# Relation maps by copies inside SBUF, ten chunks per loop turn and interleaved expert products, in a one-core attention and mixture-of-experts kernel

## The chip, the cores and the metric

One core of one Trainium2 chip runs the whole program. The metric is the device time of one execution in microseconds (us); times are medians over runs.

## What is computed

One pre-norm layer over 4096 tokens of width 256, 16 heads of 16, in fp32:

```python
q, k, v = (xn @ W.T + b for each)                      # (4096, 16, 16)
li = xn @ rel_W[:, :d].T;  lj = xn @ rel_W[:, d:].T    # 3 relations
probs = softmax(li[i] + lj[j] + rel_b)                 # per pair of tokens
bias = probs @ logical_bias.T                          # per head
gate = sigmoid(xn @ gate_W.T + gate_b)
w = softmax(q k^T / 4 + gate * bias)
x = x + (w @ v) @ Wo.T + bo
logits = layernorm(x) @ Wg;  top 2 of 8 experts, softmax over the two
x = x + sum_k weight_k * (relu(xn @ W1[e] + b1[e]) @ W2[e] + b2[e])
```

## The kernel before, in words

The program has three parts, each a block in which the five engines run lists of their own, tied by semaphores.

`project_inputs` (to 287 us) normalises x and makes q, k, v, gates and relation logits. VectorE splits q and k into two fp16 parts, and SP, the queue that issues nearly all DMAs, writes q and the coefficients to DRAM (L205, L217) and k into the stack `kst` in SBUF (L220). VectorE's third group of splits waits for all those stores (L309), since it writes over their source.

`attend` takes 32 chunks of 128 queries. A chunk has 32 steps of 128 keys (jt), and eight units of 512 keys. For a step TensorE forms the scores of two halves of eight heads in PSUM (`sc`): per half eight matmuls of q and k (L764) and eight of the relation terms (L775), the latter with the keys' relation maps `rst` as the stationary side (112 rows: high and low fp16 parts of two maps for 16 queries, and rows of ones that carry the negative row maximum) and the coefficients `cm` as the moving one. Eight blocks of 16 queries need a matmul each; block b holds queries 16b to 16b+15, so its output is, per head, a run of 16 neighbouring floats. ScalarE exponentiates (L653) and TensorE multiplies by the values (L811). In the same steps TensorE computes score maxima for later chunks (L786), two heads at a time, which VectorE reduces (L685); 16 of a chunk's 64 products are done two chunks ahead (AHEAD).

The relation maps of a chunk are 16 pieces (8 units x 2 kinds), each made by two clamps on VectorE (L677, from the key logits `dj` that SP loads per unit, L476), two exponentials on ScalarE (L631), a sum on GpSimd (L590), a logarithm and an exponential on ScalarE (L637, L639), and a rounded copy and a remainder on GpSimd (L594, L596). All 16 of a chunk are made during the chunk before; those of chunk 0 before the first scores, between the maxima products (L718 to L722). SP writes the two parts to DRAM, re-laid, in `sp_write_r` (L490) and reads a unit back in two transfers in `sp_read_r` (L500, L501) when one of the two unit buffers is free, that is when the scores before it are done (L540). GpSimd waits for the stores before it fills `rhi` again (L592). Per chunk SP also loads q (L466), sends the row maxima in eight copies (`sp_m`, L515), the output (L507) and loads the constants of the chunk after next (L480, L482).

`in_chunks` (L78) runs the chunks on every engine as a loop of 15 turns over two chunks; the last two chunks stand behind it as straight code.

`experts` adds the attention output, routes the tokens and runs 23 blocks of 512 gathered tokens. In a block TensorE does eight up products (L1344), turns the next block's tokens (L1289), and does the four output tiles of the block before (L1358), 24 matmuls each. ScalarE applies relu (L1268) and makes the high parts of the weights (L1238), VectorE splits the hidden values (L1208, L1210), splits x (L1146) and adds the bias to the output tiles (L1222), all splits of one block before the biases of the last; GpSimd makes the low parts of the weights (L1033). The output tiles have two PSUM banks, so TensorE can be two tiles ahead of VectorE.

## Time and profile before

| | us |
|---|---|
| median of 3 runs | 5311.16 |
| lowest and highest | 5309.63, 5318.84 |
| the profiled execution: its time | 5305.37 |
| its span in the trace | 5303.6 |

The page gives busy time per engine over the span: TensorE 4609.0 us, its weight loads 3497.3, VectorE 4010.2, ScalarE 3394.0, GpSimd 2102.8. A busy share is an average over stages; it says which engine a stage leans on, and the rows in order of time say who waits for whom. Durations of neighbouring matmuls overlap, so a step is read from start to start.

### The profile page before, as it was taken

What the parts mean: (1) busy time and instruction counts of PE and PEld (TensorE: products, weight loads), DVE (VectorE), ACT (ScalarE), POOL (GpSimd) and SP (SyncE); (2) the same over time, 40 slices, a digit from 0 to 9 for tenths busy, and PEclk for the clock granted to TensorE, in tenths of its full rate; (3) what the DMA queues carried; (4) which work ended last, traced back from release to release, by engine and by line L of the source; (5) the groups of instructions that cost most, each with busy time, mean ns of one, the idle gap of its engine ahead of it and who ended that gap; (6) DMA issues with size and microseconds to landing.
All of it is one profiled execution on the core that took longest, in us unless ns stands there. A gap on an engine that the chain in (4) does not pass through costs nothing. (4 is left out here: it accounts for less than half of the span.)

```text
span 5303.6 us, 184408 instructions
## 1 busy us (share of the span) xinstructions
PE 4609.0 (87%) x74128; PEld 3497.3 (66%) x74128; DVE 4010.2 (76%) x6341; ACT 3394.0 (64%) x4457; POOL 2102.8 (40%) x1811
## 2 busy tenths in 40 slices
PE   4548999999999999999999999999999983688882
PEld 3216777777777777777777777777777773466662
DVE  7288888888888888888888888888888613566663
ACT  0136877878787878787787878787878840233330
POOL 4043444444444444444444444444444413323234
PEclk8758999999999999999999999999999985789996
DMA  2634555555555555555555555555555552333323
GB/s 58 101 95 119 150 137 151 149 139 150 141 149 145 150 137 148 142 146 137 151 151 138 151 142 150 144 151 136 148 140 147 143 161 89 115 115 116 113 105 107
DMA packets 455013, 710.53 MB, mean 134 GB/s; under 512 B 138664, under 2 KB 306472, under 8 KB 425792
## 3 DMA queue, kind: packets, MB, share of 16 engines
q1 hardware_dynamic: 447936, 681.00, 47.0%
q0 software_dynamic: 6144, 16.79, 1.0%
q8 instruction: 622, 10.19, 0.8%
q14 instruction: 311, 2.55, 0.1%
HBM read 506.30 MB, written 184.93 MB: 130 GB/s over the span
## 5 line engine op out<-in xcount | busy, mean ns | idle before, releaser
L685 DVE TENSOR_REDUCE b_mxp<-b_mx 128x1 f32<-128x512 f32 x4096 | 2624.7, 683 | 541.0 <-PE b_mx L786 466.3
L653 ACT ACTIVATE b_pr<-b_sc 128x1024 f32<-128x1024 f32 x2048 | 1987.7, 1021 | 773.1 <-PE b_sc L775 772.5
L764 PE MATMUL b_sc<-b_qm,kst 128*128 128x128 f16 x16384 | 1276.4, 221 | 86.6 <-issue 82.0
L775 PE MATMUL b_sc<-b_cm,b_rst 112*128 112x128 f16 x16384 | 1275.8, 221 | 1.3 <-issue 1.3
L764 PEld LDWEIGHTS b_sc<-b_qm,kst 128*128 128x128 f16 x16384 | 977.8, 98 | 284.8 <-ACT b_pr L653 174.0
L775 PEld LDWEIGHTS b_sc<-b_cm,b_rst 112*128 112x128 f16 x16384 | 976.0, 98 | 227.7 <-issue 227.6
L811 PE MATMUL b_acc<-b_pr,vp 128*32 128x128 f32 x32768 | 1110.9, 276 | 0.5 <-issue 0.5
L811 PEld LDWEIGHTS b_acc<-b_pr,vp 128*32 128x32 f32 x32768 | 835.3, 110 | 231.6 <-ACT b_pr L653 195.4
L594 POOL CAST b_rhi<-b_ex 128x512 f16<-128x512 f32 x512 | 321.4, 628 | 1570.5 <-ACT b_ex L639 785.7
L786 PE MATMUL b_mx<-kst,b_qx 64*128 64x512 f16 x4096 | 822.8, 398 | 120.8 <-DVE b_mxp L685 116.0
L590 POOL TENSOR_TENSOR b_ex<-b_ex 128x512 f32<-128x512 f32 x512 | 658.0, 1285 | 528.7 <-ACT b_ex L631 528.1
L677 DVE TENSOR_SCALAR b_dl<-b_dj,b_const 128x512 f32<-128x512 f32 x1024 | 772.4, 756 | 5.0 <-DMA b_dj<-key_logits 3.7
L596 POOL TENSOR_TENSOR b_rlo<-b_ex,b_rhi 128x512 f16<-128x512 f32 x512 | 604.8, 1181 | 40.9
L631 ACT ACTIVATE b_ex<-b_dl 128x512 f32<-128x512 f32 x1024 | 588.2, 627 | 35.7 <-DVE b_dl L677 34.6
L786 PEld LDWEIGHTS b_mx<-kst,b_qx 64*128 64x128 f16 x4096 | 197.5, 93 | 373.4 <-DVE b_mxp L685 170.0
L1268 ACT ACTIVATE c_h<-c_ps,c_b1b 128x512 f32<-128x512 f32 x184 | 124.2, 689 | 425.1 <-PE c_ps L1344 283.2
L1358 PE MATMUL c_ps<-c_w2p,c_a 128*128 128x256 f16 x2208 | 294.6, 302 | 104.8 <-DVE c_y L1222 104.8
L637 ACT ACTIVATE b_ex<-b_ex 128x512 f32<-128x512 f32 x512 | 323.0, 631 | 91.6 <-POOL b_ex L590 91.4
L1358 PEld LDWEIGHTS c_ps<-c_w2p,c_a 128*128 128x128 f16 x2208 | 237.4, 108 | 158.3 <-DVE c_y L1222 110.9
L639 ACT ACTIVATE b_ex<-b_ex 128x512 f32<-128x512 f32 x512 | 322.3, 630 | 16.2
L1033 POOL TENSOR_TENSOR c_w1p<-c_w1r,c_w1p 128x2048 f16<-128x2048 f32 x22 | 90.2, 4100 | 448.5 <-ACT c_w1p L1238 448.5
L1344 PE MATMUL c_ps<-c_xT,c_w1p 128*128 128x512 f16 x1104 | 247.5, 385 | 11.4 <-issue 9.9
(143 smaller groups left out, 2016.8 us busy)
## 6 DMA issues: line engine op xcount, KB each, us to landing
b_dj<-key_logits SPq DMA_DIRECT2D x256, 768.0 KB, 7.5
b_rst<-relation_parts SPq DMA_DIRECT2D x256, 512.0 KB, 4.8
relation_parts<-b_rhi SPq DMA_DIRECT2D x512, 128.0 KB
relation_parts<-b_rlo SPq DMA_DIRECT2D x512, 128.0 KB
b_rst<-relation_parts SPq DMA_DIRECT2D x256, 256.0 KB, 5.3
c_w1r<-in_L_ffn_W_dram SPq DMA_DIRECT2D x23, 1024.0 KB, 4.8
c_w2r<-in_L_ffn_W_dram SPq DMA_DIRECT2D x23, 1024.0 KB, 4.8
expert_tokens<-c_zeros SPq DMA_DIRECT2D x23, 512.0 KB, 7.0
```

The source lines that it names most:

```text
L590: nc.gpsimd.tensor_tensor(ex[:, k, 0], ex[:, k, 0], ex[:, k, 1], ALU.add).then_inc(s["sum_ready"], 1)
L596: nc.gpsimd.tensor_tensor(rlo[:, k], ex[:, k, 0], rhi[:, k], ALU.subtract).then_inc(s["lo_ready"], 1)
L631: nc.scalar.activation(ex[:, k, n], dl[:, k, n], ACT.Exp, scale=sign).then_inc(s["e_ready"], 1)
L637: nc.scalar.activation(ex[:, k, 0], ex[:, k, 0], ACT.Ln, bias=1.0).then_inc(s["ln_ready"], 1)
L653: nc.scalar.activation(pr[:, jt % 2, half, :], sc[:, half].rearrange("p a b -> p (a b)"), ACT.Exp).then_inc(s["p_ready"], 1)
L677: nc.vector.tensor_scalar(dl[:, k, n], dj[:, u % 2, d], const[:, par, b:b + 1], limit, ALU.add, op).then_inc(s["d_ready"], 1)
L685: nc.vector.tensor_reduce(mxp[:, head, part:part + 1], mx[:, (bank + ab) % MX_RING, :], AX.X, ALU.max).then_inc(s["mx_used"], 1)
L764: pe.matmul(sc[:, half, side, p * P:p * P + P], kst[:, pair, jt * P:jt * P + P], qm[:, par, pair, :, side * IS:side * IS + IS], start=(p = ...
L775: ins = pe.matmul(out, rst[:, u % 2, b, j0:j0 + P], cm[:, par, half, b], start=False, stop=(b % (NB // 2) == NB // 2 - 1), skip_group_chec ...
L786: pe.matmul(mx[:, (bank + ab) % MX_RING, :], qx[rows, par, pair, :], kst[rows, pair, j0:j0 + 512], start=True, stop=True).then_inc(s["mx_r ...
L811: ins = pe.matmul(acc[32 * (h % 4):32 * (h % 4) + 32, h // 4, :], vp[:, jt, VW * h:VW * h + 32], pr[:, jt % 2, half].rearrange("p (a h i) ...
L1358: ins = pe.matmul(ps[:, 4 + d % 2, 0:D], hT[:, (b - 1) % 2, hp, f, t * P:t * P + P], w2p[:, (b - 1) % 2, wp, f, :], start=(f == 0 and hp = ...
```

## The change

In the attention part the relation maps no longer go through DRAM. GpSimd writes them into four slots, and per piece SP copies six times from SBUF to SBUF straight into `rst` (two sides of 64 queries, three row groups). The pieces are made two units ahead of their use, not a chunk ahead; chunk 0 has four made before the first scores and the rest in its steps. For the copies each block takes every fourth query of its side, so the relation matmul writes every fourth float of `sc`. The key load moves behind the copies and four units ahead, clamps run one step earlier, coefficients are loaded in two halves in unit 7, row maxima go in two copies. The loop has three turns of ten chunks; two chunks stand behind it. In the projection part six stores take the place of 48. In the experts two up products alternate with one output tile on TensorE, and VectorE's splits with the biases; the weights' high parts are made after the second and fourth relu in place of the fourth and sixth.

```diff
+R_AHEAD, D_AHEAD = 4, 3
+CLAMP_SLOT, ACC_SLOT = 0, 1
+UNROLL, LOOPS = 10, 3
...
-    with eng.Fori(0, (NT - 2) // 2) as pair:
-        chunk(pair * 2, 0, pair + 1, False)
-        chunk(pair * 2 + 1, 1, pair + 1, False)
-    chunk(NT - 2, 0, NT // 2, False)
-    chunk(NT - 1, 1, NT // 2, True)
+    with eng.Fori(0, LOOPS) as turn:
+        for n in range(UNROLL):
+            chunk(turn * UNROLL + n, n % 2, turn * (UNROLL // 2) + n // 2 + 1, False)
+    for c in range(LOOPS * UNROLL, NT):
+        chunk(c, c % 2, c // 2 + 1, c == NT - 1)
...
-                    for b in range(NB):
-                        sp.dma_start(c_dram[:, part, k].rearrange("x (i b) h -> b i x h", b=NB)[b],
-                                     t[BI * b:BI * b + BI, k]).then_inc(stored, 16)
...
+        rhi = sb("rhi", [P, 4, JU], F16)
+        rlo = sb("rlo", [P, 4, JU], F16)
...
+            for side in range(2):
+                sp.dma_start(cval[0:M_ROW, par, NB // 2 * side:NB // 2 * side + NB // 2, :],
+                             c_dram[bass.ds(x, 1)].rearrange("o a k (s i b) h -> s (o a k) i (b h)", s=2, b=NB // 2)[side]
+                             ).then_inc(s[f"cval_in{par}"], 16)
...
-        def sp_write_r(sp, x, g):
-
-            u, k = g // 2, g % 2
-            sp.wait_ge(s["lo_ready"], 16 * x + g + 1)
+        def sp_r(sp, x, u, k):
+
+            sp.wait_ge(s["lo_ready"], 16 * x + 2 * u + k + 1)
             waited(sp)
-            for part, t in ((0, rhi), (1, rlo)):
-                sp.dma_start(r_dram[bass.ds(x, 1), u, part, k].rearrange("o (i b) j -> b (o i) j", b=NB), t[:, k]).then_inc(
-                    s[f"r_out{k}{u % 2}"], 16)
-
-        def sp_read_r(sp, x, u, written):
-
-            for k in range(2):
-                sp.wait_ge(s[f"r_out{k}{u % 2}"], 32 * written)
-            waited(sp)
-            src = r_dram[bass.ds(x, 1), u].rearrange("o a k (i b) j -> (o a k i) (b j)", b=NB)
-            dst = rst[:, u % 2].rearrange("r b j -> r (b j)")
-            sp.dma_start(dst[0:64], src).then_inc(s[f"r_in{u % 2}"], 16)
-            sp.dma_start(dst[64:96], src[0:32]).then_inc(s[f"r_in{u % 2}"], 16)
+            for side in range(2):
+                for part, t in enumerate((rhi, rlo, rhi)):
+                    row = 32 * part + BI * k
+                    sp.dma_start(rst[row:row + BI, u % 2, NB // 2 * side:NB // 2 * side + NB // 2, :],
+                                 t[IS * side:IS * side + IS, 2 * (u % 2) + k, :]).then_inc(s[f"r_in{u % 2}"], 16)
...
-            for b in range(NB):
-                sp.dma_start(cval[M_ROW:M_ROW + BI, par, b], m16[BI * b:BI * b + BI, :]).then_inc(s["m_in"], 16)
+            for side in range(2):
+                sp.dma_start(cval[M_ROW:M_ROW + BI, par, NB // 2 * side:NB // 2 * side + NB // 2, :],
+                             m16[IS * side:IS * side + IS, :]).then_inc(s["m_in"], 16)
...
                 for u in range(UNITS):
-                    if u > 0 or not (isinstance(c, int) and c == 0):
-                        sp.wait_ge(s["scores_ready"], STEPS * c + max(SPU * u, 1))
-                        waited(sp)
-                    newer = 0 if last else len(range((u + 1) % 2, u - 1, 2))
-                    if u + 1 < UNITS:
-                        sp_read_r(sp, c, u + 1, UNITS // 2 * (c + 1) + newer - (1 if u == 0 else 0))
-                    elif not last:
-                        sp_read_r(sp, c + 1, 0, UNITS // 2 * (c + 1) + newer)
-                    if not last and (more or u + 1 < UNITS):
-                        sp.wait_ge(s["d_ready"], 32 * (c + 1) + 4 * u)
-                        waited(sp)
-                        sp_dj(sp, (u + 1) % UNITS)
+                    sp.wait_ge(s["scores_ready"], STEPS * c + max(SPU * u, 1))
+                    waited(sp)
                     for k in range(2):
-                        if u == 0:
-                            sp_write_r(sp, c, 2 * UNITS - 2 + k)
+                        if u + 1 < UNITS:
+                            sp_r(sp, c, u + 1, k)
                         elif not last:
-                            sp_write_r(sp, c + 1, 2 * u - 2 + k)
+                            sp_r(sp, c + 1, 0, k)
                         if u == 0 and k == 0 and not last:
                             sp_q(sp, c + 1, 1 - par)
                         if u == M_UNIT and k == 0 and not last:
                             sp_m(sp, c + 1, 1 - par)
+                    if u + 4 < UNITS or not last:
+                        sp.wait_ge(s["d_ready"], 32 * c + 4 * u + 12)
+                        waited(sp)
+                        sp_dj(sp, (u + 4) % UNITS)
                     if u == 1:
                         sp_att(sp, c)
                         if more:
                             sp.wait_ge(s["c_made"], 2 * c + 2)
                             waited(sp)
                             sp_qx(sp, c + 2, par)
-                            sp_consts(sp, c + 2, par)
+                    if u + 1 == UNITS and more:
+                        sp_consts(sp, c + 2, par)
...
-            r_stored(pool, x, u - 1, k)
+            if not (isinstance(x, int) and x == 0 and u < 2):
+                pool.wait_ge(s[f"r_in{u % 2}"], 192 * (UNITS // 2 * x + u // 2))
...
+                for turn in range(2 * UNITS):
+                    g = turn + R_AHEAD
+                    if g < 2 * UNITS:
+                        pool_r(pool, c, g)
+                    elif not last:
+                        pool_r(pool, c + 1, g - 2 * UNITS)
+                    if turn in C_MAPS and not last:
+                        pool_c(pool, c + 1, 1 - par, nth + par, C_MAPS.index(turn))
...
+                    g = jt // 2 + R_AHEAD
+                    if g < 2 * UNITS:
+                        (act_r_inv if jt % 2 else act_r_exp)(act, c, g)
+                    elif not last:
+                        (act_r_inv if jt % 2 else act_r_exp)(act, c + 1, g - 2 * UNITS)
...
-                if n % 3 == 0 and n // 3 < 2 * UNITS:
+                if n % 2 == 0 and n < 2 * R_AHEAD:
                     for k in range(2):
-                        dve_d(dve, 0, 0, 1, n // 3, k)
+                        dve_d(dve, 0, 0, 1, n // 2, k)
...
+                        if slot == CLAMP_SLOT:
+                            g, k = R_AHEAD + (jt + D_AHEAD) // 2, (jt + D_AHEAD) % 2
+                            if g < 2 * UNITS:
+                                dve_d(dve, c, par, nth, g, k)
+                            elif not last:
+                                dve_d(dve, c + 1, 1 - par, nth + par, g - 2 * UNITS, k)
...
-                side, i0 = b // (NB // 2), b % (NB // 2) * BI
-                out = sc[:, half, side, :].rearrange("p (h i) -> p h i", h=HH)[:, :, i0:i0 + BI]
+                side, part = b // (NB // 2), b % (NB // 2)
+                out = sc[:, half, side, :].rearrange("p (h i b) -> p h i b", h=HH, b=NB // 2)[:, :, :, part]
...
+                for i in range(BT):
+                    if b < NBLK:
+                        if b >= 2 and i == 0:
+                            dve.wait_ge(s["down_done"], BT * (b - 1))
+                        for f in range(i * FT // BT, (i + 1) * FT // BT):
+                            split_h(dve, b, f)
+                    if b + 1 < NBLK and i == 2:
                         split_x(dve, b + 1)
-                if b > 0:
-                    par, nth = (b - 1) % 2, (b - 1) // 2
-                    dve.wait_ge(s[f"w2_in{par}"], 32 * nth + 32)
-                    if nth:
-                        dve.wait_ge(s[f"y_out{par}"], 16 * nth)
-                    for t in range(BT):
-                        d = BT * (b - 1) + t
-                        dve.wait_ge(s["down_done"], d + 1)
-                        nc.vector.tensor_tensor(y[:, par, t], ps[:, 4 + d % 2, 0:D], b2b[:, (b - 1) % 4],
-                                                ALU.add).then_inc(s["y_done"], 1)
+                    if b > 0:
+                        add_bias(dve, b - 1, i)
 
             for g in range(GROUPS):
...
-                    if f == 3 and b + 1 < NBLK:
+                    if f == 1 and b + 1 < NBLK:
...
-                    if f == 5:
+                    if f == 3:
...
+                for i in range(BT):
+                    if b < NBLK:
+                        if i == 0:
+                            pe.wait_ge(s["w1_lo"], b + 1)
+                            pe.wait_ge(s["x_lo"], KC * (b + 1))
+                        for f in range(i * FT // BT, (i + 1) * FT // BT):
+                            up(pe, b, f)
+                    if b + 1 < NBLK and i == 1:
                         turn_x(pe, b + 1)
-                if b > 0:
-                    pe.wait_ge(s["w2_lo"], b)
-                    pe.wait_ge(s["h_split"], 2 * FT * b)
-                    for t in range(BT):
-                        d = BT * (b - 1) + t
-                        if d >= 2:
-                            pe.wait_ge(s["y_done"], d - 1)
-                        for f in range(FT):
-                            for hp, wp in parts:
-                                ins = pe.matmul(ps[:, 4 + d % 2, 0:D], hT[:, (b - 1) % 2, hp, f, t * P:t * P + P],
-                                                w2p[:, (b - 1) % 2, wp, f, :], start=(f == 0 and hp == 0 and wp == 0),
-                                                stop=(f == FT - 1 and wp == 1))
-                        ins.then_inc(s["down_done"], 1)
+                    if b > 0:
+                        if i == 0:
+                            pe.wait_ge(s["w2_lo"], b)
+                            pe.wait_ge(s["h_split"], 2 * FT * b)
```

## Rows read from the trace of the kernel before

**Rows 1.** Windows: us, busy of PE, PEld, DVE, ACT, POOL, clock, DMA.

```profile
800.00:1800.00 1000.00, 968.02 (x17753) 739.75 (x17754) 856.48 (x1346) 791.51 (x1042) 432.33 (x408) 0.99 0.54 146
...
4750.00:4809.00 59.00, 49.15 (x310) 37.10 (x309) 38.07 (x45) 20.66 (x26) 17.59 (x5) 0.91 0.33 112
```

**Rows 2.** Timeline, TensorE, chunk 30: start us, us, engine, line, operation.

```profile
4130.93 1.08 PE L811 MATMUL b_acc<-b_pr,vp 128*32 128x128 f32 x32
...
4134.59 1.08 PE L811 MATMUL b_acc<-b_pr,vp 128*32 128x128 f32 x32
```

**Rows 3.** Waits, whole span: us in total, times, longest us.

```profile
POOL b_rhi L594 <- DMA relation_parts<-b_rlo: 784.9, 218, 7.4
...
PE b_sc L764 <- issue: 82.0, 14, 6.0
```

**Rows 4.** Timeline, TensorE, expert blocks.

```profile
4770.72 10.52 PE L1344 MATMUL c_ps<-c_xT,c_w1p 128*128 128x512 f16 x48
4781.08 1.04 PE L1289 MATMUL c_ps<-c_ident,c_xb 128*128 128x128 f32 x8
...
4792.29 7.06 PE L1358 MATMUL c_ps<-c_w2p,c_a 128*128 128x256 f16 x48 [4.94 <-DVE c_y L1222]
...
4828.75 10.52 PE L1344 MATMUL c_ps<-c_xT,c_w1p 128*128 128x512 f16 x48
...
5193.96 15.89 PE L1358 MATMUL c_ps<-c_w2p,c_a 128*128 128x256 f16 x144 [1.29 <-DVE c_y L1222]
```

**Rows 5.** Timeline, TensorE, a loop turn.

```profile
1158.94 1.08 PE L811 MATMUL b_acc<-b_pr,vp 128*32 128x128 f32 x32
1166.02 1.03 PE L764 MATMUL b_sc<-b_qm,kst 128*128 128x128 f16 x8 [6.00 <-issue]
...
1170.73 1.08 PE L811 MATMUL b_acc<-b_pr,vp 128*32 128x128 f32 x32
```

**Rows 6.** Timeline, VectorE and GpSimd in one of these blocks.

```profile
4779.20 3.83 DVE L1208 CAST c_a<-c_h 128x512 f16<-128x512 f32 x1 [1.22 <-ACT c_h L1268]
4783.07 4.45 DVE L1210 TENSOR_TENSOR c_a<-c_h,c_a 128x512 f16<-128x512 f32 x1
...
4787.89 0.69 DVE L1210 TENSOR_TENSOR c_a<-c_h,c_a 128x512 f16<-128x512 f32 x1
...
4778.66 4.10 POOL L1033 TENSOR_TENSOR c_w1p<-c_w1r,c_w1p 128x2048 f16<-128x2048 f32 x1 [21.26 <-ACT c_w1p L1238]
```

**Rows 7.** Timeline, SP and VectorE in the projection stage.

```profile
128.17 17.30 SPq L205 DMA_DIRECT2D c_values<-a_chi  x32
...
136.08 0.69 DVE L313 TENSOR_TENSOR a_x_room<-a_qk,a_part_hi 128x512 f16<-128x512 f32 x1
...
200.93 0.43 DVE L311 CAST a_part_hi<-a_qk 128x512 f16<-128x512 f32 x1 [50.71 <-DMA q_stacks<-a_x_room]
```

**Rows 8.** Timeline, VectorE before the first scores.

```profile
301.49 1.22 DVE L677 TENSOR_SCALAR b_dl<-b_dj,b_const 128x512 f32<-128x512 f32 x2
```

**Rows 9.** Timeline of SP, then its issues: KB each, median us to landing.

```profile
1131.73 5.86 SPq L515 DMA_DIRECT2D b_cval<-b_m  x8
...
1162.94 2.00 SPq L466 DMA_DIRECT2D b_qm<-q_stacks  x2
...
kst<-a_part_hi SPq DMA_DIRECT2D x32, 128.0 KB, 5.4
b_cval<-b_m SPq DMA_DIRECT2D x256, 0.5 KB, 2.1
```

**Rows 10.** By line: times, duration ns min/median/max, first and last start us.

```profile
L764 PE MATMUL b_sc<-b_qm,kst x16384: 217/219/314, 425.4 to 4318.1; 128*128 128x128 f16 x200
...
L775 PE MATMUL b_sc<-b_cm,b_rst x16384: 216/219/314, 426.2 to 4318.5; 112*128 112x128 f16 x200
...
L1358 PEld LDWEIGHTS c_ps<-c_w2p,c_a x2208: 95/98/152, 4578.8 to 5209.5; 128*128 128x128 f16 x184
...
L1344 PEld LDWEIGHTS c_ps<-c_xT,c_w1p x1104: 140/143/168, 4540.8 to 5186.8; 128*128 128x128 f16 x184
```

More of the change, by code:

```diff
@@ L608, in _ @@
             pool.wait_ge(s["eye_made"], ROWS // BI + 1)
-            for g in range(2 * UNITS):
+            for g in range(R_AHEAD):
                 pool_r(pool, 0, g)
@@ L614, in chunk, with act_r_exp @@
             def chunk(c, par, nth, last):
-                if not last:
-                    for g in range(2 * UNITS):
-                        pool_r(pool, c + 1, g)
-                        if g in C_MAPS:
-                            pool_c(pool, c + 1, 1 - par, nth + par, C_MAPS.index(g))
+                for turn in range(2 * UNITS):
[6 more added lines that the diff above has]
+                        pool_c(pool, c + 1, 1 - par, nth + par, C_MAPS.index(turn))
             in_chunks(pool, chunk)
-        def act_r_exp(act, x, u, k):
-            g = 16 * x + 2 * u + k
+        def act_r_exp(act, x, n):
+            g, k = 16 * x + n, n % 2
             act.wait_ge(s["d_ready"], 2 * g + 2)
@@ L643, in _ @@
             nc.scalar.preload_act_table_set("natural_log_exp_and_others")
-            for u in range(UNITS):
-                for k in range(2):
-                    act_r_exp(act, 0, u, k)
-                    act_r_inv(act, 0, u, k)
+            for g in range(R_AHEAD):
+                act_r_exp(act, 0, g)
+                act_r_inv(act, 0, g)
             def chunk(c, par, nth, last):
@@ L725, in _ @@
                 dve_pair(dve, 1, n, 2 * PAIRN + 2 * n)
-            for k in range(2):
-                dve_d(dve, 1, 1, 1, 0, k)
+            for n in range(D_AHEAD):
+                dve_d(dve, 0, 0, 1, R_AHEAD + n // 2, n % 2)
             def chunk(c, par, nth, last):
@@ L1290, in turn_x, with up, down @@
                 ins.then_inc(s["x_turned"], 1)
+        parts = ((0, 0), (1, 0), (0, 1))
+        def up(pe, b, f):
+            n = b * FT + f
+            if n >= 4:
+                pe.wait_ge(s["relu_done"], n - 3)
+            for c in range(KC):
+                for wp, xp in parts:
+                    ins = pe.matmul(ps[:, n % 4, :], w1p[:, b % 2, wp, c, f:F:FT], xT[:, b % 2, xp, c],
+                                    start=(c == 0 and wp == 0 and xp == 0), stop=(c == KC - 1 and xp == 1))
+            ins.then_inc(s["up_done"], 1)
+        def down(pe, b, t):
+            d = BT * b + t
+            if d >= 2:
+                pe.wait_ge(s["y_done"], d - 1)
+            for f in range(FT):
+                for hp, wp in parts:
+                    ins = pe.matmul(ps[:, 4 + d % 2, 0:D], hT[:, b % 2, hp, f, t * P:t * P + P],
+                                    w2p[:, b % 2, wp, f, :], start=(f == 0 and hp == 0 and wp == 0),
+                                    stop=(f == FT - 1 and wp == 1))
+            ins.then_inc(s["down_done"], 1)
         @block.tensor
```

109 lines of the change are left out of this document (41 added, 68 removed).

## The prediction

> **What bounds the kernel now.** I read the busy time by stretch first, then the waits, then one step of TensorE in order of time. In the thousand microseconds from 800 on TensorE is busy 968, VectorE 856, ScalarE 792 and GpSimd 432, with the clock at 0.99 (the 2.4 GHz level) and the DMA engines half busy [rows 1]: attention is TensorE's. Two neighbouring steps of one chunk show the pace: the product with the values (L811) of one step starts 3.66 us after that of the step before, and nothing in between waits [rows 2]; 1024 such steps are about 3750 us of the span of 5303.6. Where TensorE does stop, the list of waits names two kinds. It waited 14 times for "issue", 5.9 us on average [rows 3], and there are 14 jumps back in a loop of 15 turns over two chunks. And GpSimd waited 785 us for the relation parts to reach DRAM [rows 3], but GpSimd is the idlest engine here and TensorE's waits don't name it: that stall goes with the change and is worth nothing by itself. The expert stage is another matter. There TensorE stands 4.94 us in every block for VectorE's bias addition (L1222), and two blocks take 58.03 us [rows 4].
>
> The profiled execution took 5305.4 us (span 5303.6), 0.1% under the median of 5311.2 us of three runs, so I subtract its durations from the median. A measurement of this kernel can tell about 0.2%, 11 us, from no change.
>
> **Loop turns.** At a turn the value products of two neighbouring steps start 11.79 us apart instead of 3.66, with 6.00 us of it "issue" and the first matmuls behind it at about double their usual time [rows 2, 5]. So a turn costs 8.1 us. Ten chunks a turn leave two jumps back of fourteen: 12 x 8.1 = 97 us. The bounds are 12 x 5.9 = 71 (the stop alone) and 100. The straight-line end of the present program, chunks 30 and 31, is where the two rows of the 3.66 us pace stand [rows 2], so long unlooped code runs at full pace.
>
> **Experts.** Today TensorE does a block's eight up products in 10.36 us, transposes (1.0 us), starts down and stops after the second output tile, because VectorE is to add the bias only after all its splits of the next hidden block. VectorE is late because two of its instructions took 3.83 and 4.45 us, beside GpSimd's weight splits of 4.1 us each; alone the second one takes 0.69 [rows 4, 6]. Alternating two up products with one down product gives VectorE the time of 5.3 us per pair of splits and one bias. TensorE's own work per block is 10.36 + 1.0 + 96 x 0.110 = 22.0 us (0.110 from the 144 last matmuls in 15.9 us) [rows 4]. VectorE is busy 38.07 us in two blocks, the long holds included: 19 a block [rows 1], still under 22. The tightest place is the x split, now put before the bias of the third tile while ScalarE copies x only after its eighth relu: going through it by these durations, x is ready about when the next block's first product wants it, and 0.2 to 1 us per block is lost. I take 22.6 against 29.0: 22 x 6.4 = 141, less about 4 at the ends, 137 us. Bounds: 95 (25 us a block) and 150. The weight splits move earlier (after f = 1 and 3); their loads are issued in the block before, some 15 us ahead, and stay covered.
>
> **Projection stage.** The coefficient stores take 32 x 0.54 us on SP, 48 of them 26 us, and then the q stores run until VectorE, 50.7 us idle, may go on at 200.93 [rows 7]. Six stores in place of 48 free 42 x 0.54 = 22.7 us of SP. But the q stores need the first eight tiles, finished at 136.8, so they start at 137 and not at 154: 17 us, and everything behind follows SP. The data moved is the same in as many pieces, and may slow the q stores: 16 us, between 5 and 23.
>
> **Start of attention.** Before the first scores VectorE works through 128 maxima with 16 pairs of clamps between them, 1.22 us a pair [rows 8]. Four pairs are left, twelve go into chunk 0, where TensorE is the bound and the same clamps ran in every chunk: 12 x 1.22 = 14.6, less one clamp that is put ahead of the first scores: 14 us, between 10 and 18.
>
> **Relation copies.** Per unit of 512 keys (four steps, 14.6 us) SP now issues 12 copies and one key load instead of six transfers and one. The nearest row to a copy inside SBUF is the 8 small ones of the row maxima, 5.86 us or 0.73 each, landing after 2.1 us; a 128 KB one lands after 5.4 [rows 9]. Twelve cost 8.8 us, and with the key load 9.3 of 14.6: SP keeps up. What is late next is the last copy of a unit. TensorE needs it 16.7 us after the buffer is free (four steps plus the part of a step that leads up to L775). In most units it lands at 12 to 13. In unit 6 it stands behind the row maxima, whose wait is now in front of it rather than behind the reads, and lands near 15. In unit 0 SP starts 3 us later (it waits for one half step more), the two loads of q (2.0 us) are between the copies [rows 9], and the sum 3.0 + 4.4 + 2.3 + 4.4 + 2.5 = 16.6 has no slack. I charge 0.3 us a chunk, 10 us; bounds 0 and 40. GpSimd's new wait, on copies of two units before, is met when it is asked. In the last chunk ScalarE now has maps to make where it had none: 2.9 us of work a step (0.79 of 3.66 [rows 1, 2]) against a TensorE step that there has no maxima products, four of 512 columns, 0.21 us each at 2.4 GHz (an estimate), so 2.8. 24 such steps give 2 us, 0 to 5. Two row-maximum copies in place of eight are behind other work.
>
> **Costed at nothing.** The key load (L476) now stands behind the copies, 10 to 13 us into a unit; VectorE's clamps want it six steps, 22 us, after the unit began, so TensorE's pace covers it until SP is 4 us behind. The loads of the constants and coefficients (three more issues) go from unit 1 to unit 7, still a chunk ahead of their use, and there SP has 5 us left. The clamps run one step earlier and ask for maps that ScalarE made two steps before. The copy of the accumulator keeps its place behind the last maxima product. If SP or VectorE lose these 4 to 5 us, the cost is rival 2's.
>
> **Sum.** 97 + 137 + 16 + 14 - 10 - 2 = 252 us: 5311 - 252 = 5059 us.
>
> **Rival 1, slower: the strided score write.** The relation matmul wrote runs of 16 neighbouring floats in PSUM and now writes every fourth float, 16 bytes apart. No row shows a matmul that does this. Two rows bound it. For nothing lost: L775 already breaks its output into runs, and its median is 219 ns, the same as L764's unbroken one [rows 10]. For a loss: on the reading side, a weight load with elements 16 bytes apart (L1344) takes 143 ns against 98 for a packed one (L1358) [rows 10]. If the write pays the same 45 ns on the engine that is the bound, 16384 x 45 ns = 737 us, and the time is 5796. It decides the sign from 252 / 16384 = 15 ns a matmul on. I take no cost, because the row of the same instruction and the same target is nearer than a load from SBUF; chance 0.16. The Trainium skill (Advanced Engine Details and Errata, PSUM Cachelines) speaks against this change: any non-contiguous access pattern is said to slow matmuls significantly, with every two neighbouring elements wanted together. By its first form L775 should be slow already, and the row says it isn't; its second form, pairs, no row here tests, and by it the result would be this rival.
>
> **Rival 2: SP becomes the clock of attention.** If a copy costs 1.2 us on SP rather than 0.73, a unit needs 12 x 1.2 + 0.8 = 15.2 us against 14.6, and unit 0 comes 5 us late: 256 x 0.6 to 32 x 5, about 150 us, time 5210. At 0.9 only unit 0 is late, by 2 us, and the time is near 5120. For it speaks that the q loads took 1.0 us each on SP [rows 9]; against it, that these copies have fixed addresses, like the row maxima's. Chance 0.13.
>
> **Rival 3: VectorE is held by GpSimd and bounds the experts.** With both long holds [rows 6] inside the x split's stretch a block takes 25 us: 22 x 2.4 = 53 less gained, 5112. Chance 0.11.
>
> **Rival 4: the loop does not do what it says.** If the stop comes back in the straight code as often as before, 97 us are missing: 5156. The pace in chunk 30 speaks against it. Chance 0.05.
>
> **Numbers.** The forecast has 0.52 and 0.03 are for what I don't see. The range takes the forecast's bounds (5311 less 290, and less about 125 when each term is poor) and rivals 2 to 4: 5020 to 5210. Left out are rival 1 and the 0.03. Faster 0.82, same 0.02, slower 0.16.
>
> **What would show it.** Right: two waits for issue of about 6 us at TensorE, 11.8 us between the value products there; first scores some 30 us earlier; no wait of L1358 for L1222 and about 22.6 us from block to block; copies of about 0.7 us each on SP; L775 still at 219 ns and a step of 3.66 us. Wrong: L775 longer or a step over 4 us (rival 1), TensorE waiting for the copied maps at the first or seventh unit (rival 2), VectorE's splits late before an up or down product (rival 3).

## The result and the profile after

The changed kernel takes 5853.6 us (median of 4 runs, 5850.5 to 5857.5) against 5312.4 of the kernel before: ratio 1.102, 95% interval [1.100, 1.104]. It is 541 us slower. The forecast was 5059, its range ended at 5210, and rival 1, the strided score write at 5796, is what happened. (A product here is one matmul of TensorE, PE in the views; PEld is its weight load.)

The windows of the changed kernel show what [rows 1] showed before; the second one is one expert block (columns as in [rows 1], then the busy share of the DMA engines and GB/s):

```profile
800.00:1800.00 1000.00, 1000.00 (x15054) 786.44 (x15054) 740.10 (x1140) 693.88 (x884) 364.10 (x345) 1.00 0.38 94
5331.76:5353.67 21.91, 21.91 (x152) 17.01 (x153) 16.68 (x23) 10.04 (x12) 8.30 (x2) 1.00 0.45 151
```

TensorE is busy all of the thousand microseconds, and 15054 products fit where 17753 did. VectorE, ScalarE, GpSimd and the DMA engines are all less busy than before, and the granted clock is no lower (1.00 against 0.99). So TensorE's own work became slower. The view by line says which of its products:

```profile
L762 PE MATMUL b_sc<-b_cm,b_rst x16384: 274/314/502, 408.6 to 5021.1; 112*128 112x128 f16 x200
...
L762 PEld LDWEIGHTS b_sc<-b_cm,b_rst x16384: 95/139/232, 408.5 to 5021.0; 112*128 112x128 f16 x200
...
L751 PE MATMUL b_sc<-b_qm,kst x16384: 219/219/395, 407.8 to 5020.3; 128*128 128x128 f16 x200
```

The score product (now L751) has its old median of 219 ns, the relation product (L762) went from a median of 219 to 314 ns [rows 10]. Durations of neighbouring products overlap, so the price is read from the timeline of TensorE, from start to start; [rows 2] have the same pair of value products before. The changed kernel:

```profile
2001.23 1.05 PE L762 MATMUL b_sc<-b_cm,b_rst 112*128 112x128 f16 x8
2002.07 0.65 PE L751 MATMUL b_sc<-b_qm,kst 128*128 128x128 f16 x8
2002.56 1.04 PE L762 MATMUL b_sc<-b_cm,b_rst 112*128 112x128 f16 x8
2003.53 0.39 PE L773 MATMUL b_mx<-kst,b_qx 64*128 64x512 f16 x2
2003.85 1.08 PE L798 MATMUL b_acc<-b_pr,vp 128*32 128x128 f32 x32
...
2008.36 1.08 PE L798 MATMUL b_acc<-b_pr,vp 128*32 128x128 f32 x32
```

The kernel before, between the two value products of [rows 2]:

```profile
4132.82 0.62 PE L775 MATMUL b_sc<-b_cm,b_rst 112*128 112x128 f16 x8
4133.28 0.61 PE L764 MATMUL b_sc<-b_qm,kst 128*128 128x128 f16 x8
4133.73 0.61 PE L775 MATMUL b_sc<-b_cm,b_rst 112*128 112x128 f16 x8
4134.27 0.39 PE L786 MATMUL b_mx<-kst,b_qx 64*128 64x512 f16 x2
```

A step is 4.51 us instead of 3.66. The two groups of eight relation products take 0.84 and 0.97 us to the next product's start, where they took 0.46 and 0.54: that is 0.81 of the 0.85 us, and the other 0.04 stand at the score group between them. Put on the 16 relation products of a step it is 0.85 / 16 = 53 ns each, which about doubles the distance between their starts. Over 1024 steps that is 870 us.

The spans add up. From the first relation product to the last the attention stage took 3892.3 us before (426.2 to 4318.5 [rows 10]) and 4612.5 now, 720 more. The stretch ahead of it is 17.6 us shorter, the stretch behind it 154.8 (985.1 before, 830.3 now): 720 - 18 - 155 = 548, and the spans differ by 547.8. The 720 is 870 less 150: from the starts of the 1024 value products I worked out how much each step takes over its ideal length (3.66 us before, 4.51 now, and 0.48 more in the one step of a chunk that holds four transposes), and the sum over the chunks fell from 161 us to 11. Below this is called the count over the ideal step. Of the 161, 112 were the loop turns, of which 10 are left; the other 49 were small waits that a slower TensorE no longer has.

### The profile page after: what moved, and what is told of

The parts are those of the page before. It is cut to its first block and busy times, and to the rows that moved or that the text cites. A ratio compares the mean times of both kernels' runs of the same rounds, so it can differ in the third digit from the quotient of the medians.

```text
span 5851.4 us, 182716 instructions
## 1 busy us (share of the span) xinstructions
PE 5392.3 (92%) x74128; PEld 4210.1 (72%) x74128; DVE 4050.4 (69%) x6341; ACT 3500.4 (60%) x4457; POOL 2087.7 (36%) x1811
## 5 line engine op out<-in xcount | busy, mean ns | idle before, releaser
L640 ACT ACTIVATE b_pr<-b_sc 128x1024 f32<-128x1024 f32 x2048 | 2098.5, 1025 | 1487.0 <-PE b_sc L762 1482.6
L762 PE MATMUL b_sc<-b_cm,b_rst 112*128 112x128 f16 x16384 | 2138.9, 310 | 0.0
L762 PEld LDWEIGHTS b_sc<-b_cm,b_rst 112*128 112x128 f16 x16384 | 1621.2, 129 | 222.9 <-issue 222.9
L751 PE MATMUL b_sc<-b_qm,kst 128*128 128x128 f16 x16384 | 1304.1, 222 | 5.7 <-issue 5.7
L751 PEld LDWEIGHTS b_sc<-b_qm,kst 128*128 128x128 f16 x16384 | 1062.4, 103 | 203.1 <-ACT b_pr L640 188.0
L579 POOL CAST b_rhi<-b_ex 128x512 f16<-128x512 f32 x512 | 312.8, 611 | 1802.7 <-ACT b_ex L627 1070.1
L663 DVE TENSOR_SCALAR b_dl<-b_dj,b_const 128x512 f32<-128x512 f32 x1024 | 824.9, 807 | 61.4 <-ACT b_ex L619 57.9
L581 POOL TENSOR_TENSOR b_rlo<-b_ex,b_rhi 128x512 f16<-128x512 f32 x512 | 593.9, 1160 | 40.9
L1307 PE MATMUL c_ps<-c_w2p,c_a 128*128 128x256 f16 x2208 | 255.4, 273 | 0.0
L1307 PEld LDWEIGHTS c_ps<-c_w2p,c_a 128*128 128x128 f16 x2208 | 216.0, 98 | 36.0
L1296 PEld LDWEIGHTS c_ps<-c_xT,c_w1p 128*128 128x128 f16 x1104 | 154.9, 145 | 87.3 <-issue 21.2
```

Source lines behind the costliest of these rows:

```text
L581: nc.gpsimd.tensor_tensor(rlo[:, slot], ex[:, k, 0], rhi[:, slot], ALU.subtract).then_inc(s["lo_ready"], 1)
L640: nc.scalar.activation(pr[:, jt % 2, half, :], sc[:, half].rearrange("p a b -> p (a b)"), ACT.Exp).then_inc(s["p_ready"], 1)
L663: nc.vector.tensor_scalar(dl[:, k, n], dj[:, u % 2, d], const[:, par, b:b + 1], limit, ALU.add, op).then_inc(s["d_ready"], 1)
L751: pe.matmul(sc[:, half, side, p * P:p * P + P], kst[:, pair, jt * P:jt * P + P], qm[:, par, pair, :, side * IS:side * IS + IS], start=(p = ...
L762: ins = pe.matmul(out, rst[:, u % 2, b, j0:j0 + P], cm[:, par, half, b], start=False, stop=(b % (NB // 2) == NB // 2 - 1), skip_group_chec ...
L1296: ins = pe.matmul(ps[:, n % 4, :], w1p[:, b % 2, wp, c, f:F:FT], xT[:, b % 2, xp, c], start=(c == 0 and wp == 0 and xp == 0), stop=(c == K ...
```

## Experiments

**Is it the write?** Theory W says that a write at every fourth float costs TensorE 53 ns a product. Theory R keeps the write innocent: copies into the product's operand now run beside it, and its weight loads went from 98 to 139 ns too. The first run puts the write back and leaves the relation term on queries that it doesn't belong to; but for that and a scale in the exponent it is the changed kernel:

```diff
-                out = sc[:, half, side, :].rearrange("p (h i b) -> p h i b", h=HH, b=NB // 2)[:, :, :, part]
+                out = sc[:, half, side, :].rearrange("p (h i) -> p h i", h=HH)[:, :, BI * part:BI * part + BI]
```

> The changed kernel with only the relation product's write put back to runs of 16 neighbouring floats, nothing else adjusted: the relation term lands on other queries, and the exponent of the scores is scaled by 1/16 to keep it finite. This is all the rest of the change without the strided write. Theory W: 5854 - 870 = about 4985 us, a step of 3.66. Theory R: 5854, the relation product at 272 ns or more. My sum of the other parts alone would give 5059.

Measured: 5042.0 us, ratio 0.949 [0.947, 0.951]. The second does the opposite, in the kernel before:

```diff
-                out = sc[:, half, side, :].rearrange("p (h i) -> p h i", h=HH)[:, :, i0:i0 + BI]
+                out = sc[:, half, side, :].rearrange("p (h i b) -> p h i b", h=HH, b=NB // 2)[:, :, :, part]
```

> The kernel before with only the write of the relation product changed to every fourth float; relation maps still go through DRAM, the loop and the experts are the old ones. The relation term lands on other queries than it should, and the exponent of the scores is scaled by 1/16 to keep it finite; the work is the same. Theory W: the relation product goes from 219 to 272 ns, the step from 3.66 to 4.51, the time from 5312 to 5312 + 1024 x 0.85 = about 6180 us, less what the loop turns' stop overlaps (6100 to 6190). Theory R: nothing changes, 5312.

Measured: 6119.6, ratio 1.152 [1.150, 1.154]. By line, the run with runs of 16:

```profile
L762 PEld LDWEIGHTS b_sc<-b_cm,b_rst x16384: 95/98/152, 406.8 to 4204.4; 112*128 112x128 f16 x200
L762 PE MATMUL b_sc<-b_cm,b_rst x16384: 216/219/314, 406.9 to 4204.5; 112*128 112x128 f16 x200
```

and the kernel before with the strided write:

```profile
L775 PEld LDWEIGHTS b_sc<-b_cm,b_rst x16384: 95/139/233, 426.3 to 5133.5; 112*128 112x128 f16 x200
L775 PE MATMUL b_sc<-b_cm,b_rst x16384: 274/314/502, 426.4 to 5133.7; 112*128 112x128 f16 x200
```

Both numbers of the changed kernel, 314 for the product and 139 for its weight load, come with the write and go with it, whatever the copies do. Theory R is dead. The second run is 805 us over its kernel before by the medians and 813 by the profiled spans; 870, less the 49 of small waits, which vanish here too, less 8 by which the turns are shorter (104 us for 112) is 813. The first run was expected 57 us lower, since 5854 - 870 forgets that those waits come back (51 us of them by the count): 5042 is what the rest of the change gives.

**How far apart may the floats be?** Two kernels change the pattern alone (with the same scale in the exponent), to pairs of neighbours with 24 bytes between, and to every second float:

```diff
-                out = sc[:, half, side, :].rearrange("p (h i b) -> p h i b", h=HH, b=NB // 2)[:, :, :, part]
+                out = sc[:, half, side, :].rearrange("p (h i b t) -> p h i b t", h=HH, b=NB // 2, t=2)[:, :, :, part, :]
...
-                out = sc[:, half, side, :].rearrange("p (h i b) -> p h i b", h=HH, b=NB // 2)[:, :, :, part]
+                out = sc[:, half, side, :].rearrange("p (h a i b) -> p h a i b", h=HH, a=2, b=2)[:, :, part // 2, :, part % 2]
```

> The changed kernel with the relation product writing pairs: two neighbouring floats, then the next pair 32 bytes on (the term lands on other queries, exponent scaled by 1/16). If neighbouring pairs are enough for full speed: the time of the run with runs of 16, about 4985 us. If each break in the run costs the same (64 breaks instead of 128), half the loss stays: about 5420. If anything short of long runs costs all: 5854.

> The changed kernel with the relation product writing every second float (8 bytes apart) instead of every fourth (the term lands on other queries, exponent of the scores scaled by 1/16). If what counts is that two neighbouring floats are written together: the full loss, 5854. If the loss grows with the distance: between 5042 and 5854, near 5450.

Measured: pairs 5036.9 (ratio 0.948 [0.946, 0.949]), every second float 5854.9 (1.101 [1.100, 1.103]). With pairs the product's row reads 216/219/314, with every second float

```profile
L762 PE MATMUL b_sc<-b_cm,b_rst x16384: 274/314/502, 408.5 to 5023.0; 112*128 112x128 f16 x200
```

Of these patterns it is a step, not a slope. 64 breaks in the run cost nothing while each piece is two floats; distances of 8 and of 16 bytes between single floats cost the same 53 ns. The second form of the rule in the Trainium skill (Advanced Engine Details and Errata, PSUM Cachelines), that neighbouring elements are wanted in twos, holds to the nanosecond; its first form, that any non-contiguous pattern slows a product, does not, by the pairs and by the runs of 16.

**Can the order be had at the other end?** The strided write was there to match queries, since the copies give each block every fourth query: one copy of 64 neighbouring partitions leaves query 4 x row + block in each block. The write can be whole if the score product reads q in that order instead, and VectorE undoes the order in its copy of the accumulator (the diff shows the read alone):

```diff
-                              qm[:, par, pair, :, side * IS:side * IS + IS], start=(p == 0), stop=False,
+                              qm[:, par, pair, :, side * IS:side * IS + IS].rearrange("p a (i b) -> p a b i", b=NB // 2), start=(p == 0), stop=False,
```

> The changed kernel with one thing different: the relation product writes runs of 16 neighbouring floats again. So that its queries still meet the right scores, the score product reads q in the order (block, row) instead of (row, block), a moving operand whose fp16 elements stand 8 bytes apart, and VectorE's copy of the accumulator puts the queries back in their order. Everything else of the change stays. Theory W (the write at every fourth float costs TensorE 53 ns a product, 0.85 us in each of 1024 steps): the step falls from 4.51 to 3.66 us and the time to 5854 - 870 = about 4985 us, if reading q at a distance of 8 bytes is free. If that read costs what the write did (the 45 ns or more per product), the time stays near 5850 and the longer product is now that of the scores. Theory R (the product is slow because copies into its operand run beside it): no change for the relation product, 5854.

Measured: 5876.1, ratio 1.106 [1.104, 1.108]. The loss moved to the other product:

```profile
L752 PEld LDWEIGHTS b_sc<-b_qm,kst x16384: 95/113/152, 405.3 to 5040.7; 128*128 128x128 f16 x200
L752 PE MATMUL b_sc<-b_qm,kst x16384: 268/288/314, 405.3 to 5040.8; 128*128 128x128 f16 x200
...
L763 PE MATMUL b_sc<-b_cm,b_rst x16384: 217/219/314, 406.2 to 5041.3; 112*128 112x128 f16 x200
```

A step is 4.53 us, 55 ns a score product more than 3.66. Single fp16 elements 8 bytes apart, as the moving operand, cost what single floats cost on the writing side. Is it pairs here as well? The write stays at runs of 16, and the diff shows the read alone:

```diff
-                              qm[:, par, pair, :, side * IS:side * IS + IS], start=(p == 0), stop=False,
+                              qm[:, par, pair, :, :].rearrange("p a (n w) -> p (a n) w", w=4)[:, :, 0:2], start=(p == 0), stop=False,
```

> The changed kernel with the relation product writing runs of 16, and the score product reading pairs of neighbouring fp16 elements, 4 bytes, one pair every 8 bytes (it reads other queries than it should, exponent scaled by 1/16). In contig_correct the read of single fp16 elements 8 bytes apart cost as much as the strided write. If pairs of elements are enough on this side too: 5042. If 4 bytes of each 8 are too little: 5850, a score product of 272 ns.

Measured: 5055.4, ratio 0.951 [0.950, 0.953]; the score product is at 217/218/314 ns. Pairs of fp16 elements, 4 bytes of every 8, are read at nearly full speed: the usual step is 3.68 us where after_contig has 3.66, about 1 ns a product and 18 us in all, which covers the 13 us between the two runs. So the loss comes from the pattern with which TensorE touches single elements. The scaled exponent has no part in it: contig_correct and the complete versions below have no such scale, and their relation products stand at 219 ns. One thing was not tried: all these writes add to what stands in PSUM already, and whether a product that only writes pays the same is open.

**The two large terms alone.** The kernel before with the new loop (`UNROLL, LOOPS = 10, 3` and the new `in_chunks`), and the kernel before with the new expert stage:

> The kernel before with only the loop changed: ten chunks in a turn and three turns. My sum: two turns left of fourteen, 97 us less: 5314 - 97 = 5217. Rival, from the profile of the changed kernel with runs of 16, where small stops of TensorE for issue of 0.6 to 3 us stand scattered through the long body: those stops belong to the long body itself and give back some 30 us: 5245. Rival 4 of the prediction (stops come back as often): 5314.

> The kernel before with only the expert stage changed: one down product after every two up products, VectorE's bias additions between its splits, weight splits earlier. My sum: 22.6 us a block instead of 29.0, 137 us less: 5177. By the block of 21.91 us in the trace of the changed kernel: 22 x (29.0 - 21.9) = 156 less, 5158. Rival 3 (VectorE held by GpSimd, 25 us a block): 5230.

Measured: loop 5233.5, ratio 0.985 [0.984, 0.987], 79 us less; experts 5156.3, ratio 0.970 [0.969, 0.972], 156 us less. The timeline of TensorE in the experts' run:

```profile
4702.94 2.75 PE L1309 MATMUL c_ps<-c_xT,c_w1p 128*128 128x512 f16 x12
4705.53 2.78 PE L1320 MATMUL c_ps<-c_w2p,c_a 128*128 128x256 f16 x24
...
4724.85 2.75 PE L1309 MATMUL c_ps<-c_xT,c_w1p 128*128 128x512 f16 x12
```

A block is 21.91 us, without a wait. In the loop's run a turn is

```profile
1630.88 1.08 PE L812 MATMUL b_acc<-b_pr,vp 128*32 128x128 f32 x32
1636.45 1.03 PE L765 MATMUL b_sc<-b_qm,kst 128*128 128x128 f16 x8 [4.49 <-issue]
1641.17 1.07 PE L812 MATMUL b_acc<-b_pr,vp 128*32 128x128 f32 x15
```

10.29 us from value product to value product. By the count over the ideal step, the turns went from 112 to 14 us, 98 saved, but all the other steps together from 49 to 72. I took this for stops of the long body itself (there are scattered ones of 0.6 to 2 us), but 15 of the 23 us stand at the 27th to 29th step of a chunk, and at the 28th TensorE waits for ScalarE's exponentials: 11 times by the profile, against 2 in the kernel before. In chunk 2 GpSimd waits 3.75 us for the row maxima at its first coefficient product (L581), ScalarE 3.03 us for the relation sum behind it (L638), TensorE 1.38 us for ScalarE. That chain comes back below; it is in the kernel before too, and why it costs more with the long loop is not shown. The 79 us lie between my sum (97) and the rival of that expectation (some 30 given back, about 69). Of the 266.5 us between the profiled spans of the kernel before (5303.6) and of after_contig (5037.1), the turns gave 100, the stretch behind attention 152.5, the stretch before it 19.3, and all other steps lost 5: 267.

**A complete version without strides in TensorE's products.** The order has to be made off TensorE's path. ScalarE writes q in the order (block, row) when it leaves PSUM in the projection stage; VectorE restores the order once per chunk in its copy of the accumulator. The bounds of the shift follow q's order (three loads of constants instead of one), and the row maxima need eight copies again instead of two:

```diff
+                    if m < 2:
+                        dst = dst.rearrange("p (s b i) -> p s i b", s=8, b=4)
+                        src = src.rearrange("p (s i b) -> p s i b", s=8, b=4)
...
+            nc.vector.tensor_copy(oT[:, :, :].rearrange("p g (s i b) -> p (g s) b i", s=2, b=NB // 2),
+                                  acc[:, :, :].rearrange("p g (s b i) -> p (g s) b i", s=2, b=NB // 2)).then_inc(s["acc_read"], 1)
```

> A complete version of the change without a strided access in any product of attention. The queries are put in the order (block, row) once, where ScalarE writes q in the projection stage; the relation maps and coefficients keep their order, so that the relation product writes runs of 16 neighbouring floats and the copies within SBUF stay 64 neighbouring partitions each. VectorE's copy of the accumulator restores the order of the outputs, the constants are loaded by three transfers instead of one, and the row maxima by eight copies again instead of two. Theory W: the time of the changed kernel with runs of 16, 5042 us, plus at most 10 for eight maxima copies in unit 6: 5040 to 5052. If a strided access anywhere else in the kernel costs (ScalarE's writes of q at 16 bytes, VectorE's copy), it shows as a longer projection stage or a longer last step of a chunk, up to 20 us more.

Measured: 5118.8, ratio 0.963 [0.962, 0.965], 67 us over the top of what was expected. The timelines of SP and of TensorE in chunk 6 show why, first SP in the seventh unit, then TensorE at the start of the eighth:

```profile
1237.59 5.59 SPq L509 DMA_DIRECT2D b_cval<-b_m  x8
1243.37 0.59 SPq L494 DMA_DIRECT2D b_rst<-b_rhi  x1
```

```profile
1249.84 1.03 PE L769 MATMUL b_sc<-b_cm,b_rst 112*128 112x128 f16 x8 [2.10 <-DMA b_rst<-b_rhi]
```

The eight maxima copies stand between the two halves of the relation copies for the eighth unit; the last half starts 5.8 us late, and TensorE waits 1.1 to 3.8 us in nearly every chunk, 62 us in the first 30 chunks. That is the place where the prediction said twelve copies would land "near 15" of 16.7 us, with two maxima copies in front. So I moved the eight behind the relation copies (`if u == M_UNIT and k == 1`):

> As runs_of_16, with one step moved on SP: in the seventh unit the eight copies of the row maxima stand behind the twelfth copy of the relation maps, not behind the sixth. In the trace of runs_of_16 TensorE waits 1.1 to 3.8 us in every chunk (62 us in all) for the last relation map of that unit, whose copies lay behind 5.6 us of maxima copies. If that order is the cause, the waits go: 5119 - 62 = 5057, up to 5062 where GpSimd's coefficient products, which then wait some 3 us longer for the maxima, delay the maps behind them. If SP has no time for 20 copies in that unit in any order, the wait only moves to the next unit: about 5119.

Measured: 5125.0, ratio 0.964 [0.963, 0.966]: no gain, where 5057 to 5062 was expected. The waits from 800 to 1800 us:

```profile
PEld b_sc L758 <- ACT b_pr L646: 63.7, 226, 4.0
...
POOL b_cm L569 <- DMA b_cval<-b_m: 36.0, 7, 6.6
ACT b_ex L631 <- POOL b_ex L579: 34.4, 14, 5.4
PE b_sc L758 <- ACT b_pr L646: 18.3, 8, 3.7
```

TensorE's wait for relation maps is gone, and a chain stands in its place: GpSimd waits for the maxima at its first coefficient product (L569), with the next relation sum (L579) queued behind; ScalarE waits for that sum with the scores' exponentials (L646) behind it; TensorE waits for those. GpSimd is the idlest engine and still set the pace here, through what stood behind its wait. One place later in GpSimd's order the maxima are there (`C_MAPS = (13, 14)`):

> As maxima_after_copies, with GpSimd's two coefficient products one place later in its order (after the maps of places 13 and 14 instead of 12 and 13). In the trace of maxima_after_copies GpSimd waits up to 6.6 us for the row maxima at the first of them; the map sum behind it comes late, ScalarE waits 3.3 us for that sum with the scores' exponentials behind it, and TensorE for those: 70 us at the 28th step and 22 at the 29th of all chunks. If this chain is the whole cause, the maxima have landed when GpSimd asks one place later, and the time falls by 80 to 90 us: 5035 to 5045. If SP is still what is late in the seventh unit (20 copies of 0.6 us and more in 14.6 us), the wait returns as a wait of TensorE for the relation maps and the time stays near 5120.

Measured: 5055.3 (5052.4 to 5069.8), ratio 0.952 [0.950, 0.953], 262 us under the kernel before and 798 under the changed one, and 10 above the top of what was expected. GpSimd's wait for the maxima is gone from that list after the first chunk, and so is the 18.3 us row of TensorE behind L646. The 28th and 29th steps, which held 97 us over the ideal step in maxima_after_copies, hold 7. A step is 3.66 us where nothing else stands in it; the one here has four transposes as well:

```profile
2098.55 1.08 PE L805 MATMUL b_acc<-b_pr,vp 128*32 128x128 f32 x32
2099.56 0.66 PE L815 MATMUL b_mx<-b_ident,b_oT 128*128 128x128 f32 x4
2100.05 0.61 PE L758 MATMUL b_sc<-b_qm,kst 128*128 128x128 f16 x8
...
2102.69 1.08 PE L805 MATMUL b_acc<-b_pr,vp 128*32 128x128 f32 x32
```

That is 4.14 us with 0.49 of transposes. The reordering is not free for the engines that do it: ScalarE's copies of q and k out of PSUM, half of them reordered, take 907 ns on average instead of 688 (L369 here, L365 in the changed kernel), VectorE's copy of the accumulator 1087 instead of 682. Little of it reaches TensorE: the last step of a chunk is 0.08 us longer, 3 us in all, and the first relation product comes at 411.6 us where after_contig has it at 406.9. This version beats both kernels.

**Loop lengths.** Two other lengths were tried, each against the version that it varies. Two chunks in a turn:

> As runs_of_16, with the loop of the kernel before: two chunks in a turn, fifteen turns. If a turn costs 8.1 us whatever else is changed and the long body is free: 12 x 8.1 = 97 more than runs_of_16, 5140. If the long body costs some 30 us in scattered stops that a short body does not have: 65 to 70 more, 5110. If the copies within SBUF are what makes the scattered stops, the stops stay with the short body too, and the difference is 97.

Measured: 5187.0, 68 more than runs_of_16. A turn mostly cost 4.5 to 5.6 us over the ideal step here, where it cost 7.8 to 8.2 in the kernel before: in the kernels whose relation maps don't go through DRAM the stop at a turn is shorter, and the saving by fewer turns smaller. The 68 us are what the expectation had for a long body that gives some 30 us back, but the count gets there otherwise: the turns cost 56 more (68 against 12, not 97 more), and the other steps gave back 13. The profiled execution is the fastest of its five, 5165, and explains 46 of the 68; the rest is not accounted for.

Six chunks in a turn:

> As maxima_after_copies, with six chunks in a turn and five turns: two more turns. At 4.6 to 6.5 us a turn, as the turns of the changed kernel cost, 9 to 13 us more. If the small stops for issue that lie scattered through the long body grow with its length, up to 10 of that comes back. So within 0 to 13 us of maxima_after_copies.

Measured: 5150.9, 26 more than maxima_after_copies where 13 at most were expected. By the count over the ideal step, the last step of the chunks, where the turns stand, gives 11 of it, the last chunk 4 and all other steps 16, half of them at the 28th step, where GpSimd's chain stands; that makes 31, and the profiled spans differ by 34. The runs of maxima_after_copies spread over 12 us and those of this one over 24. Why the other steps hold more is not explained.

## Why the prediction was wrong

**The step that failed** is the sentence in rival 1 that sets its price to nothing: "I take no cost, because the row of the same instruction and the same target is nearer than a load from SBUF". The row (L775 in runs of 16, 219 ns) was nearer in instruction and target but not in what mattered, the number of neighbours in a piece. It had 16, the changed product has one. That pairs are as good as 16 was not in that row; only the run with pairs shows it. The row that the prediction had for single elements 16 bytes apart, the weight load of L1344 [rows 10], pointed the right way. That its 45 ns stand within 8 ns of the 53 measured is in part luck: the 45 are a difference of durations, and by durations the product rose by 95; and the weight loads of L762, whose pattern did not change, went to 139 ns as well beside the slow products, so a load's duration does not tell its own pattern's price. The sum of the rival holds: from 15 ns a product on the sign turns, and 53 were measured. The chance of 0.16 was too small for a case with one row on each side.

**Point by point**, by the prediction's own terms:

| term | predicted us | measured us | from |
|---|---|---|---|
| loop turns | 97 | 101 in the changed kernel's trace, 79 alone | 112 to 10.4; before_ten_chunks |
| experts | 137 (22.6 a block) | 155 (21.91 a block) | spans; before_experts 156 |
| projection stage | 16 (5 to 23) | 6.2 | VectorE resumes at 194.75, not 200.93 [rows 7] |
| start of attention | 14 (10 to 18) | 11.4 | first relation product 17.6 earlier, less 6.2 |
| relation copies, last chunk | -12 | -5 with runs of 16, hidden in the changed kernel | count over the ideal step |
| strided write | 0, rival 737 | -870, less 49 hidden | 0.85 x 1024 |

Without the strided write the rest of the change stands at 5042.0, 17 below the forecast of 5059. Each term of the sum has the right cause and sign, but that the total comes so near is in part luck: the experts gave 18 more and the projection stage 10 less than charged, and the loop by itself gives 79, not 97. The complete version at 5055.3, 4 below the forecast, holds other work (the reordering, eight maxima copies), so that nearness says less. The term that turned the result is the one valued at nothing.

The projection term was mis-sized because the six coefficient stores are not six short ones. SP's timeline of the changed kernel:

```profile
128.21 10.92 SPq L207 DMA_DIRECT2D c_values<-a_chi  x4
139.17 5.98 SPq L207 DMA_DIRECT2D c_values<-a_clo  x2
145.19 3.51 SPq L218 DMA_DIRECT2D q_stacks<-a_part_hi  x2
```

They hold SP 17 us, 2.8 each, where the old 48 took 26 at 0.54 [rows 7]: an instruction that moves the pieces of eight holds SP 5.2 times as long, so merging them saved 9 us and not 22.7. I had cost them by the old row's time each. The q stores then start at 145.2 instead of 154.0 and lose 2.6 us of that again on the way. VectorE's wait behind them:

```profile
194.75 0.43 DVE L312 CAST a_part_hi<-a_qk 128x512 f16<-128x512 f32 x1 [44.12 <-DMA q_stacks<-a_x_room]
```

The experts' term was low by 18. Of that 22 x 0.69 = 15 are the 0.2 to 1 us a block that it charged for the tight x split, which did not occur: TensorE's own work, 22.0 us by the prediction and 21.91 measured, is the block. The copies within SBUF took SP 0.62 us each rather than 0.73, and landed after 2.5 us:

```profile
b_dj<-key_logits SPq DMA_DIRECT2D x256, 768.0 KB, 7.4
b_rst<-b_rhi SPq DMA_DIRECT2D x2048, 64.0 KB, 2.5
```

Rival 2 (SP as the clock) did not occur in the changed kernel, whose slower TensorE gives SP 18 us a unit, nor with runs of 16 at 14.6; but six more copies in one unit were enough to bring its wait (62 us), so its margin was as thin as said. Rival 3 did not occur: a block is 21.91 us, not 25. Rival 4 was true in a small part: with the loop alone, 23 of the turns' 98 us come back in other steps, most of them at the 27th to 29th.

What would have shown it wrong was stated ("L775 longer or a step over 4 us") and is what the profile has.

## What to carry to other kernels

Before a product's output or moving operand gets a new access pattern, ask how many neighbours each piece has, and look for a row with that number, not for the row of the most similar instruction; two neighbours are as good as sixteen here, and with one the products of 128 columns start 105 to 121 ns apart instead of 57 to 68. If an order of elements must change, make it where an engine off the path touches the data once. And when a wait is moved to an idle engine, follow what is queued behind it: GpSimd, busy 40% of the span, held up TensorE through ScalarE.

## What the runs showed that was not expected

- Single elements cost TensorE 53 to 55 ns per product of 128 columns on either side, written as floats 8 or 16 bytes apart or read as fp16 8 bytes apart. Pairs cost nothing on the writing side and about 1 ns on the reading side (medians 219 and 218 ns). The Trainium skill (Advanced Engine Details and Errata, SBUF Cachelines) asks for two hits in each line of 16 bytes, and fp16 elements 8 bytes apart would have them; the run with q read so, 288 ns against 219, disagrees, and the measurement decides.
- The same stop at a loop turn cost 7.8 to 8.2 us over the ideal step with the relation maps going through DRAM, about 5 with copies within SBUF at the same length of body, and 4.5 to 6.9 at ten chunks. The two differ in more than the copies, and what shortens the stop was not tried.
- A slower TensorE hides small waits: 49 us of them were gone in both kernels with the strided write. A change's loss, measured alone, is smaller than count times price.
